# A masked-attention layer and three graph layers on one core: a second output buffer, stored mask transposes, first weights split in the first batches, and another order at the hand-over

## The reference, cut to what matters

```
h = x W^T + b;  s = (h attn) h^T, masked by adj           # attention stage, per graph
x = layernorm(x + elu(softmax(s) h))
mask = adj + eye > 0
for l in 0, 1, 2:                                          # three graph layers
    sc = leaky_relu(x.aw[l,:256] + (x.aw[l,256:])^T + ab[l], 0.2), masked
    hh = layernorm(x + softmax(sc) x) * g1 + beta1
    x  = layernorm(hh + gelu(hh W1 + b1) W2 + b2) * g2 + beta2
out = layernorm(x0 + x)                                    # x0: input of the layers
```

## Time and profile before

| | |
|---|---|
| median of 3 runs | 2429.42 us (2429.07 to 2433.45) |
| profiled execution, its own time | 2421.24 us |
| its span | 2419.2 us |
| TensorE busy | 2322.8 us (96%), 16020 matmuls |
| VectorE busy | 2060.0 us (85%) |
| ScalarE busy | 1724.7 us (71%) |
| GpSimd busy | 1118.5 us (46%) |
| mean granted TensorE clock | 0.984 |
| moved by DMA | 401.71 MB |

### The profile page before, as it was taken

The page is one execution under the profiler, slowest core; times in us unless marked ns, Lnnn a source line. Parts: engine busy times, 40 slices in busy tenths (PEclk is TensorE's granted clock), DMA queues, the critical chain, the costliest instruction groups (busy, mean ns, idle before and its releaser), DMA issues.

```text
span 2419.2 us, 44992 instructions
## 1 busy us (share of the span) xinstructions
PE 2322.8 (96%) x16020; PEld 2138.7 (88%) x16020; DVE 2060.0 (85%) x4806; ACT 1724.7 (71%) x2777; POOL 1118.5 (46%) x1315
## 2 busy tenths in 40 slices
PE   7999999997799999999999999999999999999996
PEld 6998888887699999999989999999998888898996
DVE  4888888888789989989969899899887988989875
ACT  3444444444588888888868888888886878788784
POOL 3555565555234434434525455444443445555431
PEclk9999999999899999999989999999999999999998
DMA  4444445366667786676867776777685767666531
GB/s 135 142 142 154 156 155 159 111 181 156 169 172 176 183 205 179 179 188 171 194 171 174 194 191 183 203 178 180 162 224 165 178 163 193 161 180 159 139 96 44
DMA packets 399520, 401.71 MB, mean 166 GB/s; under 512 B 220545, under 2 KB 314305, under 8 KB 399297
## 3 DMA queue, kind: packets, MB, share of 16 engines
q1 hardware_dynamic: 371648, 298.17, 44.7%
q0 software_dynamic: 27648, 100.68, 17.9%
HBM read 188.77 MB, written 59.02 MB: 102 GB/s over the span
## 4 chain that ended last, share of the span: by engine, by line
PE 64%; DVE 12%; ACT 6%; DMA 5%; issue 4%; POOL 4%; SPq 4%; POOLq 0%; DVEq 0%; ACTq 0%
PE A L1764 5%; PE A L1765 5%; PE A L1766 5%; PE PT L44 5%; PE PT L46 5%; PE PT L45 5%; PE Y L1818 5%; PE Y L1820 4%; PE Y L1819 4%; SPq L951 3%; DVE t L1467 3%; PE A L44 2%; PE A L45 2%; PE A L46 2%; PE Y L652 2%
## 5 line engine op out<-in xcount | busy, mean ns | idle before, releaser
L1764 PE MATMUL A<-x_hi,pT_hi 128*128 128x258 f32 x1536 | 437.0, 284 | 22.4 <-DVE pT_lo L1474 22.3
L1818 PE MATMUL Y<-w,g_hi 128*128 128x256 f32 x1536 | 437.0, 285 | 4.8 <-DVE g_lo L1563 4.7
L1765 PE MATMUL A<-x_hi,pT_lo 128*128 128x258 f32 x1536 | 434.5, 283 | 0.0
L1766 PE MATMUL A<-x_lo,pT_hi 128*128 128x256 f32 x1536 | 432.1, 281 | 0.0
L1820 PE MATMUL Y<-w,g_lo 128*128 128x256 f32 x1536 | 430.2, 280 | 0.0
L1819 PE MATMUL Y<-w,g_hi 128*128 128x256 f32 x1536 | 430.0, 280 | 0.0
L1359 ACT ACTIVATE g<-PT,b_less 128x512 f32<-128x512 f32 x384 | 263.8, 687 | 213.5 <-PE PT L46 208.7
L1229 POOL DMA_DIRECT2D t<-maskT x192 | 173.7, 956 | 422.1 <-DVE t L1467 407.5
L1474 DVE TENSOR_TENSOR pT_lo<-t,pT_hi 128x512 fp32r<-128x512 f32 x384 | 256.7, 684 | 86.5 <-ACT t L1319 85.4
L1563 DVE TENSOR_TENSOR g_lo<-g,g_hi 128x512 fp32r<-128x512 f32 x384 | 262.7, 684 | 72.5 <-ACT g_hi L1362 71.9
L1764 PEld LDWEIGHTS A<-x_hi,pT_hi 128*128 128x128 f32 x1536 | 291.3, 190 | 30.4 <-issue 22.3
(11 more groups left out here) (162 smaller groups left out, 5896.9 us busy)
## 6 DMA issues: line engine op xcount, KB each, us to landing
t<-maskT POOLq DMA_DIRECT2D x192, 512.0 KB, 4.8
mask<-mask SPq DMA_DIRECT2D x192, 256.0 KB, 4.9
a_adj_t<-in_adj SPq DMA_DIRECT2D x64, 512.0 KB, 4.0
rrow<-rline SPq DMA_DIRECT2D x96, 256.0 KB, 4.5
x_rows<-rows SPq DMA_DIRECT2D x24, 1024.0 KB, 6.1
mask<-a_mask SPq DMA_DIRECT2D x64, 256.0 KB, 4.3
rows<-xo SPq DMA_DIRECT2D x32, 512.0 KB, 2.8
vrow<-vline SPq DMA_DIRECT2D x24, 512.0 KB, 4.3
```

The source lines that it names most:

```text
L1764: pe.matmul(L.A[:, t, 0:DE], hi, L.x_hi[:, par, j, :], start=(j == 0), stop=False)
L1765: pe.matmul(L.A[:, t, 0:DE], lo, L.x_hi[:, par, j, :], start=False, stop=False)
L1766: mm = pe.matmul(L.A[:, t, 0:D], hi, L.x_lo[:, par, j, :], start=False, stop=(j == NT - 1))
L1818: pe.matmul(L.Y[:, t, :], hi, w2_part(0, f), start=False, stop=False)
```

## The change

- The output rows xo get a second buffer (block m uses m % 2); `n2` waits for the store of block m-2.
- In the first layer each maskT half is stored to DRAM (`turned`) once it has landed; from block 16 on it is loaded from there by a plain DMA.
- In the first iteration of layers 1 and 2, two of the last three `load_split` come before the last `load_mask` and the third before `load_maskT`.
- Layer 0's weights are split like those of the other layers, in slots 2, 4, ... 16 of the attention stage (`SPLIT_AT`), stored, and loaded in slots 57 to 62 (six slices) and in `rest` (two). `first_weights`, `first_hi` and `first_lo` go. w, x_hi and x_lo become separate tiles, so that some lie in another region of SBUF.
- In the last batch the odd tiles' `values` go to J, the even to O, and wait for the tile two before.
- `score(1, 0)` and `score(1, 1)` come in slot 63's `beside` on VectorE; GpSimd's first two `add_masks` of block 1 in slot 63's; `columns`, `load_norm2` and `load_attention(1)` move into SyncE's `rest`, behind waits for `s_tm`; `shifts` and two `row_top` move later.

Tile and argument renamings (xo, x_hi, x_lo, w, `values_bank` in `scaled` and `inverse_sum`) are left out:

```diff
--- before.py
+++ after.py
...
 
+    def values_bank(b, k):
+
+        return J if b == B - 1 and k % 2 == 1 else O
+
     def bank(b, p):
...
             pe.wait_ge(s_tlo, 2 * n + 2)
-            if not start:
-                pe.wait_ge(s_z, n)
+            out = values_bank(b, k)
+            if out is J:
+                pe.wait_ge(s_z, n - 1)
+            elif not start:
+                pe.wait_ge(s_z, n if b < B - 1 or k == 0 else n - 1)
             hi, lo = pT[k % 2]
             for j in range(NT):
                 js = slice(j * P, (j + 1) * P)
-                pe.matmul(O[:, 0:DE], hi[:, js], hn[par][0][:, j, :], start=(j == 0), stop=False)
-                pe.matmul(O[:, 0:DE], lo[:, js], hn[par][0][:, j, :], start=False, stop=False)
-                mm = pe.matmul(O[:, 0:D], hi[:, js], hn[par][1][:, j, :], start=False, stop=(j == NT - 1))
+                pe.matmul(out[:, 0:DE], hi[:, js], hn[par][0][:, j, :], start=(j == 0), stop=False)
+                pe.matmul(out[:, 0:DE], lo[:, js], hn[par][0][:, j, :], start=False, stop=False)
+                mm = pe.matmul(out[:, 0:D], hi[:, js], hn[par][1][:, j, :], start=False, stop=(j == NT - 1))
             mm.then_inc(s_pv, 1)
...
     R_AT = {41: 0, 59: 1}
+    SPLIT_AT = {2 + 2 * f: f for f in range(KF)}
     TOP_AT = {24 + 2 * r if r < NT else 26 + 2 * r: r for r in range(2 * NT)}
...
                     sp.wait_ge(L.s_tm[g], 16 * k)
+                sp.wait_ge(L.s_maskT_out[half], 16 * min(k, C))
+            if k >= C:
+                sp.dma_start(L.maskT[:, HALF * half:HALF * (half + 1), :], turned[k % C, half]).then_inc(L.s_maskT[half], 16)
+                return
             r = BANK * (k % C)
             sp.dma_start_transpose(L.maskT[:, HALF * half:HALF * (half + 1), :],
                                    mask_rows[r:r + BANK, BANK * half:BANK * (half + 1)]).then_inc(L.s_maskT[half], 16)
+
+        def store_maskT(k, half):
+            sp.wait_ge(L.s_maskT[half], 16 * (k + 1))
+            sp.dma_start(turned[k, half], L.maskT[:, HALF * half:HALF * (half + 1), :]).then_inc(L.s_maskT_out[half], 16)
 
...
 
-        def raw_weights(layer, f, at, sem):
-            sp.dma_start(L.x1[:, at, :].rearrange("p (k f) -> p k f", k=KD),
+        def raw_weights(layer, f, to, sem):
+            sp.dma_start(to[:, 0, :].rearrange("p (k f) -> p k f", k=KD),
                          W1[layer, :, f * P:(f + 1) * P].rearrange("(k p) f -> p k f", p=P)).then_inc(sem, 16)
-            sp.dma_start(L.x1[:, at + 2, :], W2[layer, f * P:(f + 1) * P, :]).then_inc(sem, 16)
-
-        def first_weights(f):
-            if f >= 2:
-                sp.wait_ge(L.s_w_lo, f - 1)
-            raw_weights(0, f, f % 2, L.s_w_in[f % 2])
+            sp.dma_start(to[:, 2, :], W2[layer, f * P:(f + 1) * P, :]).then_inc(sem, 16)
 
         def load_raw(layer, f):
-            n = KF * (layer - 1) + f
-            if n == 0:
-                sp.wait_ge(L.s_w_lo, KF)
-            else:
+            n = KF * layer + f
+            if n > 0:
                 sp.wait_ge(L.s_split_out, 16 * n)
-            raw_weights(layer, f, 0, L.s_raw_in)
+            raw_weights(layer, f, L.x1 if layer > 0 else L.early, L.s_raw_in)
 
         def store_split(layer, f):
-            sp.wait_ge(L.s_raw_lo, KF * (layer - 1) + f + 1)
-            sp.dma_start(split[layer - 1, f], L.x1[:, :, :]).then_inc(L.s_split_out, 16)
+            sp.wait_ge(L.s_raw_lo, KF * layer + f + 1)
+            sp.dma_start(split[layer, f], (L.x1 if layer > 0 else L.early)[:, :, :]).then_inc(L.s_split_out, 16)
 
         def load_split(layer, f):
             if f == 0:
-                sp.wait_ge(L.s_split_out, 16 * KF * layer)
-            sp.wait_ge(L.s_ffn2, KF * (C * layer - 1) + f + 1)
-            sp.dma_start(L.w[:, f, :, :].bitcast(F32), split[layer - 1, f]).then_inc(L.s_split_in, 16)
+                sp.wait_ge(L.s_split_out, 16 * KF * (layer + 1))
+            if layer > 0:
+                sp.wait_ge(L.s_ffn2, KF * (C * layer - 1) + f + 1)
+            elif f == 0:
+                sp.wait_ge(stage.s_pv, LAST)
+            elif f == EARLY:
+                sp.wait_ge(stage.s_pv, SLOTS)
+            sp.dma_start(L.w[f][:, :, :].bitcast(F32), split[layer, f]).then_inc(L.s_split_in, 16)
 
...
                 sp.dma_start(L.ab[:, :], attn_b.partition_broadcast(P)).then_inc(L.s_ab_in, 16)
+            if slot - 1 in SPLIT_AT:
+                store_split(0, SPLIT_AT[slot - 1])
+            if slot + 1 in SPLIT_AT:
+                load_raw(0, SPLIT_AT[slot + 1])
             if slot - 1 in V_AT:
...
                     load_maskT(0, half)
-            if slot == LAST + 1:
-                columns()
-            if slot == LAST + 3:
-                load_attention(1)
-                first_weights(0)
-                first_weights(1)
+            if LAST < slot <= LAST + EARLY:
+                load_split(0, slot - LAST - 1)
+            if slot == LAST + 2:
+                for half in range(2):
+                    store_maskT(0, half)
             if slot == LAST + 4:
                 load_mask(FIRST + 2)
-            if slot == LAST + 7:
+            if slot == LAST + 6:
                 load_maskT(1, 0)
-                for f in range(2, 4):
-                    first_weights(f)
             if slot == SLOTS + NT - 2:
                 load_maskT(1, 1)
-                for f in range(4, 6):
-                    first_weights(f)
 
         def rest():
             for i in range(2):
                 sp.wait_ge(stage.s_mst[i], 16 * SLOTS // 2)
+            sp.wait_ge(L.s_tm[1], 32)
+            columns()
+            for f in range(EARLY, KF):
+                load_split(0, f)
+            sp.wait_ge(L.s_tm[3], 32)
             load_norm2(0)
+            load_attention(1)
             follow()
 
         def follow():
             for k in range(K + 2):
                 tops = tops_of(k)
-                if k == 0:
-                    for f in range(6, KF):
-                        first_weights(f)
                 if k % 2 == 0 and k < K - 2:
                     load_x(k // 2 + 1)
                 if k == 0:
                     load_r(2)
+                if k + 1 < C:
+                    for half in range(2):
+                        store_maskT(k + 1, half)
                 if 2 <= k and layer_of(k - 2) == LAYERS - 1:
...
                     load_r(2 * n)
+                if arriving:
+                    load_split(arriving, KF - 3)
+                    load_split(arriving, KF - 2)
                 for r in tops[2:]:
                     load_mask(r + MASKS)
+                if arriving:
+                    load_split(arriving, KF - 1)
                 if k + 2 < K:
                     load_maskT(k + 2, 1)
-                if arriving:
-                    for f in range(KF - 3, KF):
-                        load_split(arriving, f)
                 if k >= 2 and layer_of(k - 2) == LAYERS - 1:
...
                 pool.wait_ge(stage.s_pv, LAST)
-                for i in range(2):
-                    pool.memset(L.x_hi[:, i, :, D:D + 1].bitcast(F32), 1.0).then_inc(L.s_ones, 1)
-                    pool.memset(L.x_hi[:, i, :, D + 1:DE].bitcast(F32), 0.0).then_inc(L.s_ones, 1)
+                ones(0)
             if slot == LAST + 2:
                 row_columns(1, 1)
                 add_masks(0, range(1))
             if slot in (LAST + 3, LAST + 4, LAST + 5):
                 g = slot - LAST - 2
                 add_masks(0, range(g, g + 1))
+            if slot == LAST + 7:
+                add_masks(1, range(2))
 
         def rest():
-            add_masks(1, range(4))
+            add_masks(1, range(2, 4))
             deviation1(0)
+            pool.wait_ge(stage.s_pv, SLOTS)
+            pool.wait_ge(stage.s_t, SLOTS)
+            for i in range(2):
+                pool.wait_ge(stage.s_mst[i], 16 * SLOTS // 2)
+            ones(1)
             for k in range(1, K + 2):
...
         def n2(m):
+            xo = L.xo[m % 2]
             act.wait_ge(L.s_rs2, 4 * (m + 1))
-            if m >= 1:
-                act.wait_ge(L.s_xst, 16 * m)
+            if m >= 2:
+                act.wait_ge(L.s_xst, 16 * (m - 1))
             for t in range(TC):
-                act.activation(L.xo[:, t, :], L.Y[:, t, :], ACT.Identity, bias=L.nmr2[:, t:t + 1],
+                act.activation(xo[:, t, :], L.Y[:, t, :], ACT.Identity, bias=L.nmr2[:, t:t + 1],
                                scale=L.rstd2[:, t:t + 1]).then_inc(L.s_n2, 1)
...
 
-        def first_hi(f):
-            act.wait_ge(L.s_w_in[f % 2], 32 * (f // 2 + 1))
-            if f == 0:
-                act.wait_ge(stage.s_t, SLOTS)
-                for i in range(2):
-                    act.wait_ge(stage.s_mst[i], 16 * SLOTS // 2)
-            if f == 4:
-                act.wait_ge(stage.s_pv, SLOTS)
-            act.activation(L.w[:, f, 1:4:2, :], L.x1[:, f % 2:4:2, :], ACT.Copy).then_inc(L.s_w_hi, 1)
-
         def raw_hi(layer, f):
```

(35 more changed lines are left out.)

147 lines of the change are left out of this document (78 added, 69 removed).

## The result

Over four runs each, the changed kernel takes 2399.01 us in the median (2394.6 to 2404.83) and the kernel before 2429.24 (2419.53 to 2433.45): a ratio of 0.9891, 95% interval 0.9867 to 0.9915. The forecast was 2400.4 with a range of 2385 to 2420. The profiled execution is the longest of the four, 2404.83 us with a span of 2403.0, so the two profiles lie only 16.2 us of span apart where the medians lie 30 apart. The other 14 are the distance of the two profiled executions from their medians. Executions of one kernel differ by so much here that a good part of what follows is about where this comes from.

A forecast was written before the change was run, and what follows sets the result against it. TensorE is nearly full, so time was to be won at the hand-over, the layer boundaries and the last layer: 7 + 17.7 + 14.6 - 0.4 - 10 = 28.9, taken as 29, giving 2400.4 us, range 2385 to 2420.

The forecast's parts named there:

- Hand-over: Attention stage to layers: last mask addition 12.6 us sooner, fold's 2.0 us weights wait gone; 14.6 us gained, bounds 9 and 18.
- The 1.31 us of VectorE's idle time at 600: End of attention: VectorE's 1.31 us wait for TensorE at 600.17, to be filled by block 1's first two scores.
- Boundaries: Two layer boundaries: split weights land sooner, fold at full clock; 10.0 and 8.1 us, taken as 17.7, bounds 9.0 and 19.
- 0.8 us of the first GELU: Each layer boundary: first GELU with its table load, hidden before by slow matmuls, shows for about 0.8 us, a cost.
- the 2.1 and 1.7 us for the matmuls behind the fold: First and second boundary: with no pause, matmuls behind the fold come 2.1 and 1.7 us sooner at full clock.
- the rival on the clock: Boundaries: clock falls over the folds, matmuls behind stay slow, 4 us less; gain 25, 2404 us; chance 0.10.
- Second output buffer: Last layer: ScalarE's waits for the output store go, saving TensorE's GELU and g_lo waits, 7 us; bounds 3.8 and 17.4.
- the 16.0 us of `n2`: Last layer: ScalarE's `n2` stood nine times for the store of the one output buffer; these 16.0 us were to go.
- The 10.4 us for pT_lo: Last layer: TensorE's 11 waits for pT_lo, left in place, VectorE being behind with `final_norm` and a row maximum.
- Splits in the first batches: Attention slots 2 to 16: eight copies and subtractions lie mostly in VectorE's free time; cost 0.4 us, bounds 0 and 5.5.
- Stored transposes' price: Blocks 0 to 15: two stores ahead of raw weights' loads make ScalarE wait; cost 10 us, bounds 3 and 22.
- The rival of raw loads that drain behind the stores: First layer: raw loads land up to 3.7 us later in five half-batches, 18 us more; gain 11, 2418; chance 0.12.

The follow-up runs named there:

- again: The changed kernel itself, unchanged, run and profiled a second time: 2393.53 us, ratio 0.9854 to the kernel before.
- after: The changed kernel in its first set of runs and first profile: 2399.01 us, ratio 0.9891 to the kernel before.
- mask_behind: Changed kernel with the transpose of block 1's second mask half put back behind the columns' loads: 2400.94 us, ratio 0.9915 to the kernel before.
- old_end: Changed kernel with one PSUM bank for the last batch's values and block 1's first two scores two slots later again: 2397.34 us, ratio 0.9871.
- short_fold: Changed kernel with the fold of b2 cut from 32 matmuls to 4 in the second and third layer: 2389.35 us, ratio 0.9864.
- no_store: Changed kernel with every mask turned by the DMA transpose again and none stored: 2404.79 us, ratio 0.9892 to the kernel before.
- one_xo_no_store: Changed kernel with a single output buffer and every mask turned by the DMA transpose, none stored: 2415.06 us, ratio 0.9970.
- splits_behind: Changed kernel with a layer's last three split weights loaded behind the last masks and the mask load two blocks on again: 2398.66 us, ratio 0.9911.
- raw_ahead: Changed kernel with a half-batch's two transposed-mask stores moved behind its raw weights' and first two mask rows' loads: 2391.08 us, ratio 0.9832.
- both: Changed kernel with mask stores behind the raw weights' loads, and three 128-byte stores ahead of first-half transposes, blocks 2 to 15: 2381.9 us, ratio 0.9812.

## Why the prediction was right, and where it was not

The total, 29 us of gain forecast and 30 measured (35.5 for again, in its set), is right, and in part by luck. The two profiled executions gained 16.2 and 33.7 us of span; the 10 us put on the stores lie between the 20.6 and the 4.9 that the first layer lost in them, and while the hand-over gained a little more than its term, the boundaries gained less.

*Hand-over*, forecast 14.6: 15.1 in the profile of after, 17.1 in again. Its steps hold almost to the number: last addition at 611.67 for 611.8, pause before aggregate(1) 4.35 us for 4.7, up-projection at 632.09 for 632 to 634. That SyncE's queue is the larger part is shown by mask_behind (8 to 10 us). The 1.31 us of VectorE's idle time at 600 that the second bank and the early scores were to use was not seen: old_end loses nothing.

*Boundaries*, forecast 10.0 and 8.1: 8.5 and 5.4 (8.5 and 4.7 in again). The two add up to 18.1; the sum took 17.7 without saying why, and no row had a price for its 0.8 us of the first GELU. The weights' wait went, all of it in after and all but 2.2 us in again, and the first fold ran 3.70 us for a forecast 3.5. The step that failed is the 2.1 and 1.7 us for the matmuls behind the fold: they stay slow, and the second fold itself took 5.3 us. I had put the low clock of the earlier trace rows down to the pause; short_fold, against after and again, shows that it comes with the 32 narrow matmuls even behind a pause of under 0.4 us, so the rival on the clock named the right place. A long pause still counts: the five folds that waited 3.4 us or more (two before, one each in no_store, one_xo_no_store and splits_behind) took 6.96 to 6.99 us, the lower level throughout. Boundaries and second layer together gained 15.1 us (13.9 in again) for the 17.7 of the sum; the rival had put 4 us on it. The sentence of the Trainium skill from which I took that rival (TensorE: Matmul & The Clock Gate, the paragraph on transpose mode) is about transposes; these run before the fold in short_fold too, with the clock full, so they are not what decides here.

*Second output buffer*, forecast 7: the last layer gained 6.6 to 7.6, but not by the buffer alone. I read the 16.0 us of `n2` as one cause. It had two, a single buffer and a store behind a transpose, and the change removed both. The 10.4 us for pT_lo stayed as forecast (9.9 in 11 waits).

*Splits in the first batches*: from 20 to 540 us TensorE did 3267 matmuls before, 3265 in after and 3282 in again, so a cost of 0.4 us is too small to be seen, and one of 5.5 us, some 35 matmuls, is excluded.

*Stored transposes' price*, forecast 10 us, bounds 3 and 22: 20.6 in one profile, 4.9 in the next. The failed step is that of the landing: I used one row of 8.5 us for every transpose. In the profile of after the second halves land after about 8 us in one half-batch and 4 to 5 in the next (7.8 at 746.97, 4.2 at 785.55), so that the raw weights were late in half-batches 4, 6, 8 and 10 and not in 5, 7 and 9; and now and then one takes 11 to 16 us. The rival of raw loads that drain behind the stores holds for some of them. In the five kernels that have no store ahead of these loads (before, no_store, one_xo_no_store, raw_ahead, both) none of the first layer's took over 6.4 us to land. Behind stores, one pair of eight took 9.0 and 8.8 us in after and two pairs 6.7 to 7.6 us in again, each issued 0.3 to 0.4 us behind a store that itself took 7.2 to 8.4 us; the other 13 pairs landed in 3.8 to 5.7 us. That is less than the 3.7 us in five half-batches on which the rival counted; the rest of ScalarE's waits comes from loads that are issued late. The price is not that of moving the stored bytes: no_store without them has 581.9 us in the first layer, again with them 583.0, and both, with them, 576.9. It is their place in the queue, ahead of the raw loads, and the very late transposes. Whether the stores make the near coincidences more frequent, by moving the start of the transposes, stays open; no_store and one_xo_no_store have them as well. The 10 us between again and both (ratios 0.9854 and 0.9812) divide at raw_ahead: by ratio (0.9832) about evenly, by medians into 2.5 and 9.2 us, with intervals that overlap at each step; the small stores alone, without raw_ahead's edit, were not tried.

## What to carry to other kernels

When runs of one program spread more than its stages explain, profile it twice and cut both profiles at the same landmarks; a stretch that differs shows where to look, which no view of one execution does. Before a gain is given to one edit of a change that removes two obstacles to the same transfer, undo each alone and both together. A wait on an event is also a choice of when a transfer starts, and a small piece of work behind it can be worth more than the earliest start.

## What the runs showed of the hardware

A DMA transpose (512 KB, SyncE's queue) and an accumulating DMA (512 KB, GpSimd's queue) that start within about 0.2 us of each other make the transpose land after 14 us in the median (23 cases) instead of 7 (510), and an 8 KB store behind it took 12.4 us instead of 3.2. Further apart they do not, save for four at 650 to 654 us that took over 11 us for a cause not looked into. In the two profiles in which they were kept apart, in two different ways, no transpose after 660 us took over 9.5 us; as again has none either, what carries this is the count and the narrow spread of both's runs more than these two profiles; by what mechanism the two get in each other's way, no run here shows. The Trainium skill (DMA: Bandwidth & Descriptors, Rules for kernel authors) says that a transpose beside ordinary DMAs needs nothing; that is said of correct data, and of time the rows above show the contrary.

TensorE's clock fell to its lower level (0.50) behind 32 matmuls of two columns, with no idle time between, and also with a 512-column matmul after every fifth or sixth; behind four of them it stayed at 1.00.
